# Second cross-attention of a two-layer decoder: its scores moved to the end of the odd slots, and the row minima of four heads taken together at the head of the next slot

## The chip, the cores and the metric

One core of a Trainium2 chip runs the whole program; the other cores are idle. The metric is the device time of one execution in microseconds, as a median over runs. Five engines work side by side, each through its own list of instructions in order: TensorE (PE, with its weight loads PEld), VectorE (DVE), ScalarE (ACT), GpSimd (POOL) and SyncE (SP), which issues the DMAs. They meet only at semaphores. Matmul results go to PSUM, which has eight banks; VectorE and ScalarE read them from there.

## The reference, cut to what matters

A decoder of two layers works on x of 8 batch rows x 256 positions x 512 and a context of the same shape. Each layer has a self-attention, an attention on the context and a feed-forward part, each followed by a residual addition and a layer norm. The change lies in the second layer's attention on the context, for a batch row:

```python
q = _w8a8_linear(x, wq, bq).reshape(B, N, H, D).transpose(0, 2, 1, 3)     # H = 16 heads, D = 32
k = (cond @ wk.T + bk).reshape(B, L, H, D).transpose(0, 2, 1, 3)
v = (cond @ wv.T + bv).reshape(B, L, H, D).transpose(0, 2, 1, 3)
scores = jnp.einsum('bhnd,bhld->bhnl', q, k) * inv_sqrt_d + mask[:, None]
attn = jax.nn.softmax(scores, axis=-1)
o = jnp.einsum('bhnl,bhld->bhnd', attn, v)
return _w8a8_linear(o.transpose(0, 2, 1, 3).reshape(B, N, C), wo, bo)
```

`_w8a8_linear` rounds its input by rows and its weights to whole steps of 1/127 of their largest value, multiplies, and scales back. For one batch row the scores of a head are 256 x 256.

## The kernel before, in words

The stage is `cross1`. Its work is written as a plan: a list of slots, eight for each batch row j, and in each slot a list of pieces of work. `put(slot, order, what, j, i)` places a piece; inside a slot the pieces stand by their order number. Every engine walks the same plan and, for each piece, issues its own instructions of it, or none. So one order number sets the place of a piece in all five queues. Work on row j is prepared in the slots before `base = 8 * j` (keys, rounded queries, projection, values), its attention runs in slots `base` to `base + 8`, and its output is finished up to slot `base + 17`. In a steady slot, pieces of three batch rows thus lie side by side.

The names that matter, with their lines in the profile, for row j:

- `scores` (TensorE, L2488): 24 small matmuls for four heads, into PSUM banks 0 to 3, which always hold scores. They need the exponentials of the four heads before (`s_exp`), which read the same banks. They stand in the odd slots.
- `soft`, for two heads i: VectorE adds the mask and takes the row minimum of the negated scores (L2710, four instructions and four reads of the accumulator), ScalarE takes the exponential with the minimum as bias and sums it (L2592, four). It stands in every slot.
- `flip`, for two heads: TensorE transposes the exponentials into two banks (L2501, eight), ScalarE copies them out (L2603, one instruction, 128x1024). It stands one slot behind its `soft`.
- `pv` ("attended", L2513, 16 matmuls for four heads), with ScalarE's copy (L2609); `fin` (L2523, transposes of the attended values) and `quotient` (VectorE, L2723); `round_o`, `turn_o` (L2532, copy L2615), `out` (L2542) and `out_end` (VectorE, L2742, then GpSimd).
- `key`, i = 0 to 3 (L2439, 12 matmuls), `key_high` (ScalarE, L2570), `key_low` (VectorE, L2673); `value` (L2451, 12 matmuls) and `value_out` (VectorE, L2682); `round` (VectorE, L2628 and two small ones, then GpSimd), `turn` (L2461, copy L2577), `scale` (L2424) and `scale_out` (L2662), `project` (L2472) and `project_out` (VectorE, L2696, then GpSimd).
- `n1` to `n4`: the layer norm of four tiles after every second batch row (statistics L200, normalising L232).

In the steady part the odd slot after an even one holds, besides soft, flip and scores (m is a whole number): slot 8m+1 `project_out`, `key_low`, `out`, `pv`, `key`; slot 8m+3 `project_out`, `key_low`, `fin`, `pv`, `quotient`; slot 8m+5 `value_out`, `turn_o`, `pv`, `scale`; slot 8m+7 `value_out`, `out`, `pv`, `key`. The even slots: 8m `round`, `key_low`, `key`, `project`; 8m+2 `key_low`, `key`, `project`; 8m+4 `round_o`, `value`, `turn`; 8m+6 `scale_out`, `value`.

PSUM banks other than those of the scores are handed out by `Rooms`, at build time, in the order of the plan: a piece that takes a bank waits (`left`) for the reader of the piece that had it last. Four banks serve flips and everything else, and a flip takes two. Worked out for the steady part this gives, among others: the flip of an odd slot (even i) waits for the copy of the flip one slot before; `out` in slot 8m+1 and `fin` in slot 8m+3 take the bank of the flip in their own slot and wait for its copy, and so does the `pv` of slots 8m+1 and 8m+5, and the `key` of slot 8m+7; `project` in slot 8m takes the bank of key 0 and waits for its `key_low`, which stands in the same slot; `project` in slot 8m+2 waits for the `key_low` of key 2, in that slot too; `out` in slot 8m+7 waits for `scale_out`, and the `pv` there for `value_out`.

Of the kernel before, what the change touches and what calls it, by code (L numbers as in the profile page):

```python
# [2201 lines left out]
def cross1(K):  # L2202
# [5 lines left out]
    J, U = 8, 4  # L2208
# [46 lines left out]
    def put(slot, order, what, j, i=0):  # L2255
        at.setdefault(slot, []).append((order, len(at), (what, j, i)))
# [10 lines left out]
    for j in range(J):  # L2267
        base = 8 * j
        put(base - 16 if j != 1 else -11, 6 if j != 1 else 8, "context", j)
        put(base - 16 + (j == 2), 3, "round", j)  # L2270
        first = 3 if j == 0 else -3 if j == 1 else 0
        put(base - 13 if j else 2, 6 if j else 8, "bias", j)
        put(base - 12 - first, 5, "turn", j)
        put(base - 12 - first, 9, "turned", j)
        put(base - 11 - first, 5, "scale", j)
        put(base - 10 - first, 3 if j != 1 else 1.6, "scale_out", j)
        for i in range(4):
            put(base - 9 + i - (5, 0, 0)[min(j, 2)], 5, "key", j, i)
            put(base - 8 + i - (5, 0, 0)[min(j, 2)], 1.5, "key_high", j, i)
            put(base - 8 + i - (5, 0, 0)[min(j, 2)], 4, "key_low", j, i)  # L2280
        for i in (0, 1):
            put(base - 8 + 2 * i if j else i - 10, 5, "project", j, i)
            put(base - 7 + 2 * i if j else i - 9, 2 if j == 0 else 1.7 if j == 1 else 3, "project_out", j, i)
            put(base - 6 + 2 * i if j else i - 8, 3 if j else 2.2, "project_low", j, i)
            put(base - 4 + 2 * i if j else i - 8, 5 if j else (5.5, 2)[i], "value", j, i)
            put(base - 3 + 2 * i if j else -7, 3 if j else 9, "value_out", j, i)
        put(base - 4 if j else -16, 6, "mask", j)
        for i in range(8):
            if U == 2 or i % 2 == 0:
                put(base + i - 1 if j or i else -7, 2.5, "scores", j, i // (U // 2))  # L2290
            put(base + i, 1, "soft", j, i)
            put(base + i + 1, 2, "flip", j, i)
        for g in range(4):
            put(base + 2 * g + 3, 5, "pv", j, g)
            put(base + 2 * g + 3, 9, "pv_out", j, g)
        put(base + 11, 5, "fin", j)
        put(base + 11, 9, "quotient", j)
        put(base + 12, 3, "round_o", j)
        put(base + 13, 5, "turn_o", j)
        put(base + 13, 9, "turned_o", j)  # L2300
        for i in (0, 1):
            put(base + 15 + (2 * i if j < 7 else 0), 5, "out", j, i)
            put(base + 15 + (2 * i if j < 7 else 0), 9, "out_end", j, i)
        if j % 2:
            for i, what in zip({5: (24, 24, 25, 26), 7: (16, 16, 16, 16)}.get(j, (22, 23, 26, 29)), ("n1", "n2", "n3", "n4")):
                put(base + i, 3, what, j)
# [314 lines left out]
    def vector(e):  # L2621
# [12 lines left out]
        for slot in plan:  # L2634
            for what, j, i in slot:
# [54 lines left out]
                elif what == "project_out":  # L2690
# [5 lines left out]
                        last = e.scalar_tensor_tensor(out=QF[:, m, :], in0=PS[:, b, 256 * (m % 2):256 * (m % 2) + 256],  # L2696
                                                      scalar=swI[:, m:m + 1], in1=sxB[:, :], op0=ALU.mult, op1=ALU.mult)
                    last.then_inc(p_dq.sem, 1)
                elif what == "soft":
                    n = 8 * j + i  # L2700
                    if i == 0:
                        e.wait_ge(*mk_neg.upto(j + 1))
# [182 lines left out]
    K.at_context, K.at_weights, K.at_split, K.at_exps = at_context, at_weights, at_split, at_exps  # L2885
    K.context_read, K.scores_made = x_lo.upto(J - 2), s_in.upto(16 // U * J)
    return Stage(last - first, banks, tensor, scalar, vector, gpsimd, sync)


# [344 lines left out]
def decoder(nc, d, out):  # L3234
    with ExitStack() as ctx:
# [5 lines left out]
        K.rooms, rooms = Rooms(), K.rooms  # L3241
        a1 = whole(attention1(K))
        x1 = cross1(K)
        e1 = experts1(K)
        stages = [first, a0, c0, e0, a1, x1, e1]
# [88 lines left out]
```

## Time and profile before

| | before |
|---|---|
| median of 3 runs | 2325.73 us (2324.29 to 2326.95) |
| the profiled execution's own time | 2325.44 us |
| its span | 2323.7 us |
| mean granted clock of TensorE | 0.96 |
| TensorE matmuls | 2099.0 us busy, 90% of the span |
| VectorE | 1274.0 us, 55% |
| ScalarE | 1036.9 us, 45% |
| GpSimd | 890.5 us, 38% |

The span is the time from the first to the last instruction in the profile; the execution's own time has 1.7 us more around it. The stage with the change lies at the end: its scores run from 1921.7 to 2232 us. Busy times of matmuls are modelled and overlap a little, so the time that a group of matmuls costs is best read as the distance from its start to the start of the next. A bracket behind a row of the timeline is the engine's idle time before it and the instruction whose end released it.

### The profile page before, as it was taken

The numbers are of one execution on the slowest core, as the hardware profiler recorded it, in microseconds if no ns is written. First come the engines' busy times: TensorE is split into PE (matmuls) and PEld (weight loads), VectorE is DVE, ScalarE is ACT, GpSimd is POOL, SyncE is SP. The second block draws the span as 40 slices with busy tenths as digits, with TensorE's granted clock in tenths as the row PEclk, the third lists the DMA queues.
The fourth block names the chain that finished last, engine by engine and source line by source line (L and its number), as shares of the span: only waits on it lengthen the run. The fifth ranks groups of instructions, "written<-read, shape, count | busy, mean of one in ns | idle before, by whom it ended". The sixth has DMA issues, their size and how long they took to land.

```text
span 2323.7 us, 37777 instructions
## 1 busy us (share of the span) xinstructions
PE 2099.0 (90%) x13677; PEld 1668.7 (72%) x13677; DVE 1274.0 (55%) x3279; ACT 1036.9 (45%) x2324; POOL 890.5 (38%) x944
## 2 busy tenths in 40 slices
PE   7799999899999987999999999968999877888877
PEld 6688888687777866887777788856565446667645
DVE  2554445554555455644537521146787756667767
ACT  3332333444434433444543322234666545677753
POOL 1753444334343322214433025434545335445302
PEclk9899999899999998999999999988999978999988
DMA  3302101111111111111111011103423310000001
GB/s 128 137 32 68 46 33 50 46 42 46 49 46 46 37 39 63 34 35 53 46 37 37 19 37 55 46 19 59 64 49 59 101 64 15 15 28 6 15 1 73
DMA packets 58312, 109.05 MB, mean 47 GB/s; under 512 B 7184, under 2 KB 35088, under 8 KB 54672
## 3 DMA queue, kind: packets, MB, share of 16 engines
q1 hardware_dynamic: 58128, 106.63, 15.6%
q8 instruction: 111, 1.82, 0.3%
q14 instruction: 73, 0.60, 0.1%
HBM read 86.10 MB, written 4.26 MB: 39 GB/s over the span
## 4 chain that ended last, share of the span: by engine, by line
PE 43%; DVE 10%; ACT 6%; issue 3%; POOL 2%; DMA 0%; SPq 0%; ACTq 0%; DVEq 0%; POOLq 0%
PE PS L1330 18%; ACT xP L2592 3%; PE PS L1827 3%; PE PS L1923 3%; PE PS L1346 2%; DVE aM L2063 2%; PE PS L1891 1%; DVE st L200 1%; DVE PS L2710 1%; PE PS L2451 1%; PE PS L993 1%; PE PS L2488 1%; PE PS L1911 1%; PE PS L1005 1%; PE PS L1878 1%
## 5 line engine op out<-in xcount | busy, mean ns | idle before, releaser
L1330 PE MATMUL PS<-WH,bXH 128*128 128x512 f32 x640 | 258.4, 404 | 0.0
L1330 PE MATMUL PS<-WH,bXL 128*128 128x512 f32 x640 | 250.2, 391 | 0.0
L1330 PE MATMUL PS<-WL,bXH 128*128 128x512 f32 x640 | 250.2, 391 | 0.0
L2063 DVE TENSOR_REDUCE aM<-PS 128x4 f32<-128x1024 f32 x128 | 153.8, 1221 | 55.2 <-PE PS L1891 53.9
L1627 POOL TENSOR_TENSOR mixed<-mixed,s 128x256 f32<-128x256 f32 x112 | 82.3, 739 | 234.1 <-DVE s L1528 234.0
L1632 POOL TENSOR_TENSOR WL<-sg,WH 128x512 fp32r<-128x512 f32 x80 | 101.9, 1304 | 181.7 <-ACT WH L1446 181.7
L421 PE MATMUL PS<-aXH,QKH 128*128 128x512 f32 x384 | 157.2, 409 | 14.9 <-ACT sq L634 7.9
L421 PE MATMUL PS<-aXH,QKL 128*128 128x512 f32 x384 | 153.0, 398 | 0.0
L421 PE MATMUL PS<-aXL,QKH 128*128 128x512 f32 x384 | 152.9, 398 | 0.0
L2002 ACT ACTIVATE aPT<-PS 128x1024 f32<-128x1024 f32 x128 | 128.6, 1024 | 49.4 <-PE PS L1911 48.6
L721 DVE TENSOR_TENSOR qkL<-PS,qkH 128x512 fp32r<-128x512 f32 x96 | 65.9, 690 | 142.7 <-ACT qkH L598 142.7
L1330 PEld LDWEIGHTS PS<-WH,bXH 128*128 128x128 f32 x640 | 120.5, 188 | 28.6 <-issue 2.0
L1330 PEld LDWEIGHTS PS<-WH,bXL 128*128 128x128 f32 x640 | 120.4, 188 | 26.5
L1330 PEld LDWEIGHTS PS<-WL,bXH 128*128 128x128 f32 x640 | 120.7, 189 | 22.6
L690 DVE TENSOR_TENSOR xN<-PS,xN 128x512 f32<-128x512 f32 x128 | 88.2, 691 | 78.0 <-PE PS L454 75.6
L794 POOL TENSOR_SCALAR E<-lgB,lgS 128x256 f32<-128x256 f32 x64 | 73.2, 1144 | 150.2 <-DVE aT L747 140.7
L2592 ACT ACTIVATE xP<-PS,xM 128x256 f32<-128x256 f32 x256 | 118.0, 481 | 24.6 <-DVE xM L2710 24.6
L747 DVE TENSOR_TENSOR aT<-sq,E 128x512 f32<-128x512 f32 (+1 forms) x128 | 81.6, 678 | 82.3 <-ACT sq L634 43.6
L1528 DVE SCALAR_TENSOR_TENSOR s<-s,cf,PS 128x256 f32<-128x256 f32 x112 | 53.9, 481 | 127.5 <-ACT s L1464 125.4
L598 ACT ACTIVATE qkH<-PS 128x512 fp32r<-128x512 f32 x96 | 57.1, 598 | 140.2 <-PE PS L421 140.2
L1511 DVE SCALAR_TENSOR_TENSOR s<-s,PS 128x256 f32<-128x256 f32 x80 | 33.7, 421 | 149.1 <-ACT s L1462 149.0
L804 POOL TENSOR_TENSOR E<-E,DM 128x256 f32<-128x256 f32 x64 | 45.9, 738 | 180.2 <-ACT E L609 180.2
(407 smaller groups left out, 6069.2 us busy)
## 6 DMA issues: line engine op xcount, KB each, us to landing
sg<-in_gu SPq DMA_DIRECT2D x16, 1024.0 KB, 4.8
gQK<-in_Wqk SPq DMA_DIRECT2D x16, 768.0 KB, 6.2
gC<-in_Wc SPq DMA_DIRECT2D x16, 512.0 KB, 6.4
lgB<-gate_sums SPq DMA_DIRECT2D x32, 256.0 KB, 4.6
aqs<-aQH SPq DMA_DIRECT2D x64, 128.0 KB, 4.3
xN<-in_xT SPq DMA_DIRECT2D x4, 1024.0 KB, 11.7
xN<-in_x SPq DMA_DIRECT2D x4, 1024.0 KB, 7.4
cst<-in_cT SPq DMA_DIRECT2D x8, 512.0 KB, 3.9
```

Source lines behind the costliest of these rows:

```text
L421: mm = e.matmul(PS[:, b, :], w[:, kc, 128 * m:128 * m + 128], x[:, kc, c:c + 512], start=kc == 0 and i == 0, stop=kc == KC - 1 and i == 2)
L690: e.tensor_tensor(xN[:, t, :], PS[:, b, :], xN[:, t, :], ALU.add).then_inc(o_add.sem, 1)
L747: at = e.tensor_tensor(aT[:, j, c:c + w].rearrange("p (h q) -> p h q", h=2), sq[:, c:c + w].rearrange("p (h q) -> p h q", h=2), E[:, j:j + ...
L794: e.tensor_scalar(E[:, j, 0:256], lgB[:, n % 2, 256 * j:256 * j + 256], lgS[:, c0:c0 + 1], 0.0, ALU.subtract, ALU.min)
L1330: mm = e.matmul(PS[:, b, :], x[:, kc, c:c + 128], y[:, kc, :], start=kc == 0 and n == 0, stop=kc == KC - 1 and n == 2)
L1627: e.tensor_tensor(mixed[:, i, :], mixed[:, i, :], s2[tick % 2][:, :], ALU.add).then_inc(t_add.sem, 1)
L1632: last_ = e.tensor_tensor(WL[w % 2][:, kc, :], sg[:, kc, :], WH[w % 2][:, kc, :].bitcast(F32), ALU.subtract)
L1827: mm = e.matmul(PS[:, b, 0:256], w[:, kc, 128 * m:128 * m + 128], x[:, kc, :], start=kc == 0 and k == 0, stop=kc == KC - 1 and k == 2)
L1923: mm = e.matmul(PS[32 * r:32 * r + 32, b, :], V[y][:, kt, 4 * i + r, :], PT[:, (n + 2 * (r // 2) + kt) % 8, r % 2, :], start=kt == 0, stop ...
L2002: e.activation(PT[:, n % 8, :, :], PS[:, b:b + 2, :], ACTF.Exp, scale=0.25).then_inc(t_exp.sem, 1)
L2063: e.tensor_reduce(M[j % 2][:, :, :].rearrange("x q (h c) -> x h q c", h=2)[:, :, :, i], PS[:, b:b + 2, :].rearrange("p h (q k) -> p h q k" ...
L2592: last = e.activation(P[:, i % 2, a, q, :], PS[:, r, 256 * q:256 * q + 256], ACTF.Exp, bias=M[y][:, q, h:h + 1], scale=-1.0, accum_out=den ...
```

## The change

Three order numbers in the plan and one name. `scores` gets 9.5 in place of 2.5, so that it stands last in its odd slot (the very first scores of the stage stay where they are). The minima of VectorE leave `soft` for a piece of their own, `max`, which stands for both i of an even and odd pair at 0.2 at the head of the even slot: VectorE takes the minima of four heads in one go. `key_high` of keys 0 and 2 from the third batch row on gets 0.6, ahead of the exponentials. ScalarE's part of `soft` stays.

```diff
--- before.py
+++ after.py
@@ -2276,7 +2276,7 @@
         put(base - 10 - first, 3 if j != 1 else 1.6, "scale_out", j)
         for i in range(4):
             put(base - 9 + i - (5, 0, 0)[min(j, 2)], 5, "key", j, i)
-            put(base - 8 + i - (5, 0, 0)[min(j, 2)], 1.5, "key_high", j, i)
+            put(base - 8 + i - (5, 0, 0)[min(j, 2)], 0.6 if j >= 2 and i % 2 == 0 else 1.5, "key_high", j, i)
             put(base - 8 + i - (5, 0, 0)[min(j, 2)], 4, "key_low", j, i)
         for i in (0, 1):
             put(base - 8 + 2 * i if j else i - 10, 5, "project", j, i)
@@ -2287,7 +2287,8 @@
         put(base - 4 if j else -16, 6, "mask", j)
         for i in range(8):
             if U == 2 or i % 2 == 0:
-                put(base + i - 1 if j or i else -7, 2.5, "scores", j, i // (U // 2))
+                put(base + i - 1 if j or i else -7, 9.5 if j or i else 2.5, "scores", j, i // (U // 2))
+            put(base + i - i % 2, 0.2, "max", j, i)
             put(base + i, 1, "soft", j, i)
             put(base + i + 1, 2, "flip", j, i)
         for g in range(4):
@@ -2696,7 +2697,7 @@
                         last = e.scalar_tensor_tensor(out=QF[:, m, :], in0=PS[:, b, 256 * (m % 2):256 * (m % 2) + 256],
                                                       scalar=swI[:, m:m + 1], in1=sxB[:, :], op0=ALU.mult, op1=ALU.mult)
                     last.then_inc(p_dq.sem, 1)
-                elif what == "soft":
+                elif what == "max":
                     n = 8 * j + i
                     if i == 0:
                         e.wait_ge(*mk_neg.upto(j + 1))
```

In slot 25, for instance, the order was soft, key_high, flip, scores, project_out, key_low, out, pv, key, out_end, pv_out. It becomes soft, key_high, flip, project_out, key_low, out, pv, key, out_end, pv_out, scores.

## Rows read from the trace of the kernel before

**Rows 1.** Stretch: us, busy PE, PEld, DVE, ACT, POOL, clock, DMA; slots 15 to 55.

```profile
2009.00:2202.90 193.90, 170.86 (x1732) 134.36 (x1732) 137.49 (x480) 137.84 (x419) 92.90 (x89) 1.00 0.05 17
```

**Rows 2.** Waits, 1923 to 2240 us; waited for: us, times, longest.

```profile
PE PS L2488 <- ACT xP L2592: 26.8, 26, 3.0
```

**Rows 3.** Timeline of TensorE (start, us, engine, line; wait before in brackets).

```profile
2056.55 0.39 PE L2488 MATMUL PS<-xKH,xQH 32*128 32x256 f32 x4 [0.77 <-ACT xP L2592]
...
2057.84 1.04 PE L2542 MATMUL PS<-ow,oT 128*128 128x512 bf16 x4 [0.30 <-ACT xPT L2603]
...
2059.80 0.38 PE L2439 MATMUL PS<-xXH,xWKH 128*128 128x256 f32 x1
...
2062.12 0.36 PE L2439 MATMUL PS<-xXH,xWKH 128*128 128x256 f32 x1
...
2064.52 1.04 PE L2501 MATMUL PS<-idF,xP 128*128 128x128 f32 x8
...
2066.31 0.39 PE L2488 MATMUL PS<-xKH,xQH 32*128 32x256 f32 x4 [0.75 <-ACT xP L2592]
...
2067.59 1.09 PE L2523 MATMUL PS<-idF,xnT 128*128 128x128 f32 x8 [0.30 <-ACT xPT L2603]
...
2070.59 0.48 PE L2451 MATMUL PS<-xWVH,xXH 128*128 128x512 f32 x1
...
2075.28 1.09 PE L2501 MATMUL PS<-idF,xP 128*128 128x128 f32 x8 [0.80 <-ACT qxT L2577]
...
2077.10 0.39 PE L2488 MATMUL PS<-xKH,xQH 32*128 32x256 f32 x4 [0.73 <-ACT xP L2592]
...
2086.26 0.39 PE L2488 MATMUL PS<-xKH,xQH 32*128 32x256 f32 x4 [0.99 <-ACT xP L2592]
...
2095.68 0.39 PE L2488 MATMUL PS<-xKH,xQH 32*128 32x256 f32 x4 [0.78 <-ACT xP L2592]
...
2117.00 0.39 PE L2488 MATMUL PS<-xKH,xQH 32*128 32x256 f32 x4 [0.73 <-ACT xP L2592]
...
2125.22 0.39 PE L2488 MATMUL PS<-xKH,xQH 32*128 32x256 f32 x4
```

**Rows 4.** Timeline of ScalarE.

```profile
2060.64 0.47 ACT L2592 ACTIVATE xP<-PS,xM 128x256 f32<-128x256 f32 x1 [0.25 <-DVE xM L2710]
...
2064.33 0.47 ACT L2592 ACTIVATE xP<-PS,xM 128x256 f32<-128x256 f32 x1 [0.48 <-DVE xM L2710]
...
2066.14 0.48 ACT L2570 ACTIVATE xKH<-PS,bk 128x256 fp32r<-128x256 f32 x1
...
2066.49 1.04 ACT L2603 ACTIVATE xPT<-PS 128x1024 f32<-128x1024 f32 x1
```

**Rows 5.** Timeline of VectorE.

```profile
2059.68 0.42 DVE L2710 CUSTOM_DVE_ANT_0 PS<-PS,xmk 128x256 f32<-128x256 f32 x1
...
2079.63 2.47 DVE L200 BATCH_NORM_STATS2 st<-xN 128x6 f32<-128x512 f32 x4
...
2090.51 1.22 DVE L2628 TENSOR_REDUCE sx<-xN 128x2 f32<-128x1024 f32 x1
...
2092.33 0.49 DVE L2673 SCALAR_TENSOR_TENSOR xKL<-PS,bk,xKH 128x256 fp32r<-128x256 f32 x1 [0.20 <-ACT xKH L2570]
...
2113.99 3.67 DVE L232 TENSOR_SCALAR xN<-xN,mv,ny 128x512 f32<-128x512 f32 x4
```

**Rows 6.** Timeline of TensorE behind a long wait.

```profile
1988.08 0.59 PE L2488 MATMUL PS<-xKH,xQH 32*128 32x256 f32 x4 [3.01 <-ACT xP L2592]
...
1993.20 1.09 PE L2501 MATMUL PS<-idF,xP 128*128 128x128 f32 x8
```

**Rows 7.** Timeline of TensorE, scores of slots 51, 55 and 61.

```profile
2183.92 0.39 PE L2488 MATMUL PS<-xKH,xQH 32*128 32x256 f32 x4 [0.88 <-ACT xP L2592]
...
2202.89 0.39 PE L2488 MATMUL PS<-xKH,xQH 32*128 32x256 f32 x4 [0.55 <-ACT xP L2592]
...
2231.28 0.39 PE L2488 MATMUL PS<-xKH,xQH 32*128 32x256 f32 x4 [1.85 <-ACT xP L2592]
```

## Prediction

> **What bounds the kernel now.** I read the stretches first, then the waits, then the timeline of one pass over a batch row (j), engine by engine. Between 2009 and 2203 us the second cross-attention is in its steady pattern and TensorE is busy 88% of the time at full clock [rows 1]: near its bound, with short pauses. The waits say where: its scores wait for ScalarE's exponentials, 26.8 us in 26 waits over the stage [rows 2], and the exponentials in turn wait for VectorE's minima [rows 4]. The timeline shows the loop. Starts of scores lie 9.76, 10.79, 9.16 and 9.42 us apart (slots 25, 27, 29, 31, 33); the 9.16 is 8.22 where no layer norm stands in it (2117.00 to 2125.22) [rows 3]. In one such pair of slots: scores take some 0.93 us; the output product follows, which VectorE must drain before it looks at minima; the minima begin at 2059.68, 3.1 us after the scores began; four exponentials; again minima; four exponentials to 2066.14; then the next scores at 2066.31 [rows 3 to 5].
>
> The second thing to see is the 0.30 us wait of TensorE right behind scores, at 2057.84 and 2067.59, for the PSUM copy of the flip [rows 3]. The product that stands there (out, or fin) takes the bank that the flip just before the scores has filled. ScalarE copies that bank only behind the slot's own four exponentials and a key's high part: exponentials 2064.33 to 2066.14, copy 2066.49, TensorE free at 2067.59 [rows 3, 4]. The 0.93 us of scores, plus the wait, exactly cover this copy. That cover is what the edit takes away.
>
> **The change, part by part.** No instruction is added or removed and no DMA; only orders change. (The bank plan follows flip, key, project and so on, whose order among each other stays, so every bank is the same as before.) I walk each kind of slot pair from T = 0, the end of scores, with durations of rows 3 to 5. Common head: minima begin at 0.1; exponentials of the even slot start when the first head's two minima are out, 0.96 later (2059.68 to 2060.64 [rows 4, 5]), so 1.07; four, 1.81 (2064.33 to 2066.14 [rows 4]), end at 2.88. All eight minima at 0.38 end at 3.16 instead of 1.6, which is the price of taking four heads together. The copy of the odd flip runs 2.88 to 3.93. The odd slot's exponentials no longer wait for minima: 3.93 to 5.74. A key's high part 0.36, the copy of the even flip 1.04. So TensorE may pass the bank at 7.2 with a key in the slot and at 6.84 without. Moving the high part of keys 1 and 3 of four ahead of the exponentials costs nothing: ScalarE is idle there.
>
> Slots 8m+2, 8m+3: TensorE's flip 0.8, key and project 2.4 (2062.12 to 2064.52), flip again end about 5.3 (project waits for VectorE's low part until 3.6). Then it stands until 7.2; fin and attended 2.0 (out and attended are 1.96, 2057.84 to 2059.80), scores 0.93: 10.15. Before 9.76. **+0.4**, five times, one with 0.3 more: 2.3.
>
> Slots 8m+4, 8m+5: flip 0.8, then value and turn 4.69 to the next flip with its wait (2070.59 to 2075.28, the wait for the turned copy stays as ScalarE again gets there behind the odd copy): flip ends 6.2. Copy of the even flip: exponentials 5.28 to 7.1, copy to 8.15. Attended, scale product, scores: 10.6. Before 10.79. **-0.2**, three times. Where the four normalising passes of 3.67 us [rows 5] stand ahead of the value copy, VectorE now starts them 1.5 us later against the same TensorE work: 11.9, or +1.2 once. Together 0.6.
>
> Slots 8m+6, 8m+7: copy of the even flip done at 6.79, key 1.51, scores: 9.3 against 8.2, **+1.0**, twice. With a norm's statistics (2.47 [rows 5], and I put 1.0 for its small steps and the scale's copy) VectorE, already held until 3.16 by eight minima, releases the scale at 6.7 and the value at 8.2: 11.6 against 9.16, +2.4, twice. Together 6.8. The two pairs of slots 52 to 55, 18.97 us now [rows 7], hold normalising passes and no key: 11.4 + 7.7, +0.2.
>
> Slots 8m, 8m+1: the worst. Project takes the bank of the key just before, which is freed by that key's low part, and VectorE has in front of it eight minima (to 3.16) and the rounding scale (from 2090.51, so that the low part came at 2092.33 [rows 5]; 1.6 of it is the scale), so project runs from 5.2 instead of 2.3. Then project 0.9, flip 0.8 with its 0.2 of latency, copy 7.2 to 8.25, out and attended 1.96, key 1.5, scores 0.93: 12.6 against 9.42. **+3.2**, five times: 16.0.
>
> The steady part sums to 2.3 + 0.6 + 6.8 + 0.2 + 16.0 = +25.9. In the first fifteen slots the same walk gives losses of the same kinds and gains where odd minima stood behind long VectorE work (the 3.01 us wait at 1988.08 [rows 6]); I take +1.5, bounds -5 and +8. In the tail there is little for TensorE to do and out and attended leave the loop: 28.39 us for three pairs [rows 7] become 24.5 (6.9, 8.8, 8.8). Behind the last scores both exponential groups end 5.7 later by the head above, where now two copies of the turn and one of attended stand before them; I estimate 2.7 gained. Sum at full clock: 25.9 + 1.5 - 3.9 - 2.7 = +20.8.
>
> **The clock.** Waits of up to 1 us never lowered it in the steady part [rows 1, 3]. A wait of 3.01 us at 1988.08 did: scores, fin and attended up to the flip at 1993.20 took 5.12 [rows 6] against 2.95 for the same three, so 2.2 us. The changed slots 8m, 8m+1 have one wait of 2.9 us and another of 1.3, six times with the one at slot 8. I take the fall each time: 6 x 2.1 = +12.6 (2.1 because project and flip, not all of the later work, run slow). Bounds: nothing, or every kind of pair that gets waits of 1.4 and 1.9 us as well, some 10 more at 1.5, +28 in all.
>
> The Trainium skill (TensorE: Matmul & The Clock Gate, section "A second HAM failure mode: psum-queue depth-cycling") tells of a kernel in which frequent small pauses between groups of matmuls, while banks are recycled, made the clock swing between its two levels, at a cost to throughput. The steady part here has such pauses and stays at 1.00, so as it stands the rule is not borne out; with pauses two to three times as long it speaks against the change, and is the second rival.
>
> Total +33.4 on the profiled execution's own time of 2325.44 (span 2323.7 and 1.7 around it; the median of three is 2325.73, 0.3 above): **2359 us**.
>
> **Rivals.** (1) The same walk, but the clock holds: +21, 2346. For it: the two waits of slots 8m, 8m+1 are parted by work of 1.7 us. Chance 0.2. (2) The clock swings in all pairs with pauses: 21 + 28 = +49, 2374. For it: two waits in each such pair; against it: waits of 1.4 to 1.9 us are half of the one that lowered it. 0.13. (3) Faster: TensorE's waits for exponentials go and nothing takes their place. Place: the bank that out and fin take. Price: -26.8, 2299. It decides if ScalarE gets through eight exponentials, a copy, a key and another copy (7.2 us from the scores' end) before TensorE has worked off the even slot and a flip, which needs 4.1 to 6.2 us by rows 3; so it would need ScalarE a third faster. Against it too: the present 0.30 waits. 0.06. (4) The gains of earlier odd exponentials balance the losses, because VectorE's minima overlap better than I have it: within 5 us. 0.06. My own case has 0.55.
>
> Slower by over 0.2% (4.7 us, about what a measurement of this kernel can tell from no change): 0.88; within: 0.06; faster: 0.06. Range: from the case where project is not held (pairs 8m at 11.5, no clock fall: +21 - 6.6, 2340) with something for the start of the stage, 2336, up to rival 2 with a little more, 2380.
>
> **What would show it.** In the changed trace: no wait of scores for exponentials in the steady part; instead out, fin and attended wait for the flip's copy, 1.5 to 2.5 us each in slots 8m+2, and 1.3 in 8m; project waits about 3 us for the key's low part in slots 8, 16, 24, 32, 40, 48; starts of scores 12.6 (14.7 with the clock down), 10.15, 10.6, 9.3 us apart; ScalarE's odd exponentials follow the copy without a gap; TensorE's busy share in the steady part down from 88% to about 78%; granted clock below 1.00 there. The stage's tail, from slot 55, shorter. The prediction is wrong if out and fin find their bank free, if the low part comes in time, or if the clock stays at 1.00 (then only the last term falls).

## The result and the profile after

The changed kernel takes 2369.01 us (median of 4 executions, 2366.80 to 2370.77) against 2325.01 us (4 executions, 2324.11 to 2326.95) for the kernel before. The ratio is 1.0185, 95% interval 1.017 to 1.02: slower by 44.0 us. The profiled execution has a span of 2369.0 us, against 2323.7.

In kernel.py of the changed kernel every line from the plan on stands one line further down, so its number is one higher: scores L2489, flip L2502, project L2473, out L2543, the exponentials L2593, the copy of a flip L2604, `key_low` L2674, the minima L2711. First the stretches, as in [rows 1]: slots 15 to 55.

```profile
2015.97:2249.54 233.57, 182.89 (x1707) 140.96 (x1716) 133.34 (x480) 137.68 (x417) 93.03 (x88) 0.93 0.04 13
```

The same instructions fill 233.57 us instead of 193.90. TensorE is busy 78% of it (182.89 / 233.57; 88% before), and its clock is 0.93 instead of 1.00. Its busy time itself grew by 12 us, though no matmul was added. The growth lies in the pairs of slots whose clock was below 1.00: slots 24, 25 were busy 8.63 us before and are busy 10.08 us now, at 0.88. GpSimd and ScalarE are busy for the same time as before, VectorE for 4 us less.

Second, what TensorE waited for between 1923 and 2290 us (us in total, times, longest):

```profile
PE PS L2473 <- DVE xKL L2674: 26.1, 13, 2.8
PE PS L2502 <- ACT xP L2593: 8.5, 4, 2.2
PE PS L2524 <- ACT xPT L2604: 8.0, 6, 1.5
PE PS L2543 <- ACT xPT L2604: 7.8, 6, 1.7
PE PS L2514 <- ACT xPT L2604: 7.4, 8, 1.6
```

The 26.8 us of scores behind exponentials [rows 2] are gone, to the last one. In their place project waits 26.1 us for a key's low part, and out, fin and attended wait 23.2 us for the copy of a flip.

Third, the timeline of TensorE over the pair of slots 24, 25 and the first half of the next, to be laid beside [rows 3]:

```profile
2060.68 0.39 PE L2489 MATMUL PS<-xKH,xQH 32*128 32x256 f32 x4
...
2066.93 1.89 PE L2473 MATMUL PS<-qxT,qw 128*128 128x256 bf16 x8 [2.81 <-DVE xKL L2674]
2068.61 1.59 PE L2502 MATMUL PS<-idF,xP 128*128 128x128 f32 x8
2071.61 0.81 PE L2543 MATMUL PS<-ow,oT 128*128 128x512 bf16 x3 [1.40 <-ACT xPT L2604]
...
2074.97 0.39 PE L2489 MATMUL PS<-xKH,xQH 32*128 32x256 f32 x4
...
2079.57 1.05 PE L2473 MATMUL PS<-qxT,qw 128*128 128x256 bf16 x8 [1.16 <-DVE xKL L2674]
...
2082.99 1.09 PE L2524 MATMUL PS<-idF,xnT 128*128 128x128 f32 x8 [1.50 <-ACT xPT L2604]
```

Project and the flip behind it in slot 24 of the kernel before, which [rows 3] don't have:

```profile
2053.86 1.05 PE L2472 MATMUL PS<-qxT,qw 128*128 128x256 bf16 x8
2054.74 1.04 PE L2501 MATMUL PS<-idF,xP 128*128 128x128 f32 x8
```

The changed kernel's stretch on VectorE and on ScalarE:

```profile
2061.85 0.43 DVE L2711 CUSTOM_DVE_ANT_0 PS<-PS,xmk 128x256 f32<-128x256 f32 x1 [2.84 <-PE PS L2489]
...
2064.88 1.21 DVE L2629 TENSOR_REDUCE sx<-xN 128x2 f32<-128x1024 f32 x1
...
2066.41 0.47 DVE L2674 SCALAR_TENSOR_TENSOR xKL<-PS,bk,xKH 128x256 fp32r<-128x256 f32 x1
```

```profile
2060.85 0.47 ACT L2571 ACTIVATE xKH<-PS,bk 128x256 fp32r<-128x256 f32 x1 [1.21 <-PE PS L2440]
2062.84 0.48 ACT L2593 ACTIVATE xP<-PS,xM 128x256 f32<-128x256 f32 x1 [1.52 <-DVE xM L2711]
...
2064.66 1.03 ACT L2604 ACTIVATE xPT<-PS 128x1024 f32<-128x1024 f32 x1
2065.56 0.49 ACT L2593 ACTIVATE xP<-PS,xM 128x256 f32<-128x256 f32 x1
...
2070.30 1.02 ACT L2604 ACTIVATE xPT<-PS 128x1024 f32<-128x1024 f32 x1 [2.42 <-PE PS L2502]
```

Read them from the end of scores, at 2061.60. VectorE works through eight minima to 2064.88, then through the rounding scale, and gets to the low part of the key at 2066.41. Project takes the bank that this instruction frees and stands still for 2.81 us. ScalarE's exponentials of the odd slot follow its copy without a gap (2065.56), and it is done with them at 2067.4 and with a key's high part at 2067.9. Then it waits 2.42 us for the flip, which is late because project was. So the two waits of TensorE are in series, and the rows of project and flip (1.89 and 1.59 in place of 1.05 and 1.04) show the clock at the lower of its levels between them.

The starts of scores lie 14.29 (slots 24, 25), 10.04, 10.82, 12.84, 16.75 and 12.54 us apart, against 9.40, 9.76, 10.79, 9.16, 9.42 and 10.54 before.

### The profile page after: what moved, and what is told of

Its sections match the earlier page's. It is cut to its first block, busy times and chain, and to the rows that moved or that the text cites. A ratio compares the mean times of both kernels' runs of the same rounds, so it can differ in the third digit from the quotient of the medians.

```text
span 2369.0 us, 37756 instructions
## 1 busy us (share of the span) xinstructions
PE 2112.5 (89%) x13663; PEld 1676.6 (71%) x13677; DVE 1267.2 (53%) x3279; ACT 1038.7 (44%) x2324; POOL 893.2 (38%) x944
## 4 chain that ended last, share of the span: by engine, by line
PE 43%; DVE 10%; ACT 5%; issue 4%; POOL 2%; SPq 1%; DMA 1%; ACTq 0%; DVEq 0%; POOLq 0%
PE PS L1330 17%; PE PS L1923 3%; PE PS L1827 3%; PE PS L1346 2%; DVE st L200 2%; DVE aM L2063 1%; ACT xP L2593 1%; DVE PS L2711 1%; PE PS L1891 1%; PE PS L2502 1%; PE PS L2514 1%; PE PS L2440 1%; ACT xPT L2604 1%; PE PS L2489 1%; PE PS L993 1%
## 5 line engine op out<-in xcount | busy, mean ns | idle before, releaser
L421 PE MATMUL PS<-aXH,QKH 128*128 128x512 f32 x384 | 157.1, 409 | 15.4 <-ACT sq L634 7.9
L2711 DVE CUSTOM_DVE_ANT_0 PS<-PS,xmk 128x256 f32<-128x256 f32 x256 | 99.4, 460 | 96.8 <-PE PS L2489 96.8
L2593 ACT ACTIVATE xP<-PS,xM 128x256 f32<-128x256 f32 x256 | 118.5, 488 | 50.5 <-PE PS L2502 32.9
```

The lines of the kernel that those rows point to most:

```text
L421: mm = e.matmul(PS[:, b, :], w[:, kc, 128 * m:128 * m + 128], x[:, kc, c:c + 512], start=kc == 0 and i == 0, stop=kc == KC - 1 and i == 2)
L2593: last = e.activation(P[:, i % 2, a, q, :], PS[:, r, 256 * q:256 * q + 256], ACTF.Exp, bias=M[y][:, q, h:h + 1], scale=-1.0, accum_out=den ...
L2711: last = e.tensor_tensor_reduce(out=s, in0=s, in1=mk[y][:, q, :], scale=1.0, scalar=3.0e38, op0=ALU.add, op1=ALU.min, accum_out=M[y][:, q, ...
```

## The experiments

Each change below is against the changed kernel or the kernel before, as said; diffs show the plan's lines. Ratios are to the kernel before, measured on the same chip.

### 1. low_first: `key_low` ahead of the minima

Added to the changed kernel.

```diff
-put(base - 8 + i - (5, 0, 0)[min(j, 2)], 4, "key_low", j, i)
+put(base - 8 + i - (5, 0, 0)[min(j, 2)], 0.1 if j >= 2 and i % 2 == 0 else 4, "key_low", j, i)
```

> The changed kernel with one order number more: key_low of keys 0 and 2 (from the third batch row on) at 0.1, ahead of the four heads' minima on VectorE. If the project of slots 8m is held by VectorE's queue, as the walk has it, these pairs (14.3 to 14.5 us in the changed kernel, one 16.75) become 11.6, slot 35 falls from 12.5 to about 10.9, slots 8m+2 stay at 10.0, and the whole is some 20 us shorter than the changed kernel: 2349. If only the PSUM copies hold TensorE, the wait moves behind the flip and the time stays at 2369; if the clock falls as before in spite of the shorter wait (2.4 in place of 2.8 us), about 2358.

Measured: 2362.56 us, ratio 1.0158 (1.0143 to 1.0173). Project's wait is gone from slots 24, 25, but those slots still take 13.34 us. The timeline of TensorE there, scores' end at 2056.71:

```profile
2059.07 1.05 PE L2473 MATMUL PS<-qxT,qw 128*128 128x256 bf16 x8
2060.86 1.09 PE L2502 MATMUL PS<-idF,xP 128*128 128x128 f32 x8 [0.73 <-ACT xPT L2604]
2063.96 1.69 PE L2543 MATMUL PS<-ow,oT 128*128 128x512 bf16 x4 [2.01 <-ACT xPT L2604]
2065.58 1.94 PE L2514 MATMUL PS<-xPT,xV 128*32 128x256 f32 x16
```

The stretch from scores to scores, with its clock:

```profile
2055.80:2069.14 13.34, 10.59 (x93) 7.20 (x92) 7.08 (x24) 6.82 (x21) 7.28 (x8) 0.87 0.01 2
```

What follows: out stands until 7.25 us behind the scores' end, where ScalarE's four exponentials, copy, four exponentials, high part and copy end (7.2 in the prediction). ScalarE's row of work is a second limit right behind VectorE's, and removing the first alone saves about 1 us a pair, where 2.7 to 2.9 were expected. Behind the 2.01 us wait the clock was down too: out and attended took 1.69 and 1.94. In slots 8, 9 of the same execution, where it stayed at 1.00, the pair took 11.33 us, near the 11.6 of the walk.

### 2. fill_wait: work put where project waits

Added to the changed kernel: key 1 of a row (from the third row on) multiplies its 12 products three times over into its bank, so 24 matmuls more in slots 8m, with the same result. They lie in the stretch where project would wait.

```diff
-for kc in range(KC):
+for _ in range(3 if j >= 2 and i == 1 else 1):
+    for kc in range(KC):
```

> The changed kernel, but TensorE does the 12 matmuls of key 1 in slots 8m three times into the same bank (the same result), which fills 2.8 us of the 2.8 us wait for the key's low part; nothing else is moved. If the fall of the clock behind this wait is a cost of its own, the pairs of slots 8m go from 14.3 to 12.6 us (the one of 16.75 too), and the kernel is some 10 to 13 us faster than the changed one in spite of 2.8 us more matmul work in each: 2357. If the clock has no part in it: 2369 or a little more.

Measured: 2361.94 us, ratio 1.0151 (1.0136 to 1.0166): with 24 matmuls more in each of six batch rows it is some 7 us faster than the changed kernel, where 10 to 13 were expected. Slots 24, 25:

```profile
2056.29:2069.23 12.94, 11.77 (x117) 9.81 (x117) 6.97 (x24) 6.92 (x21) 6.88 (x7) 1.00 0.01 2
```

The clock is at 1.00 and the pair takes 12.94 instead of 14.29, near the 12.6 of the walk. In none of the six filled pairs did it fall. So without the wait there was no fall, and one fall costs about 1.4 us a pair. Part of the gain was lost again in slots 46 to 51 (13.35, 12.85 and 13.04 against 11.80, 11.77 and 10.89): the clock was at 0.87 in the first and at 0.77 in the last of them, and in slot 48 the changed kernel's project waits only 1.29 us, so the added matmuls found no wait long enough there.

### 3. scores_early: the changed kernel with scores back at 2.5

```diff
-put(base + i - 1 if j or i else -7, 9.5 if j or i else 2.5, "scores", j, i // (U // 2))
+put(base + i - 1 if j or i else -7, 2.5, "scores", j, i // (U // 2))
```

> The changed kernel with the scores back at 2.5 in their odd slot; the minima of four heads together and the early key_high stay. If scores last is what loses the cover of the flip's copy, the waits of out and fin go back to 0.3 us or less, slots 8m+2 take about 9.1 us (9.76 in the kernel before, because the odd exponentials no longer wait for minima), slots 8m about 10.0 (9.42 before, the key's low part is late), the others as before, and the time is 2325 within 5. If the minima together are the cause of the loss: 2350 or more.

Measured: 2321.25 us, ratio 0.9981 (0.9972 to 0.9991). The whole loss is gone. The waits of out and fin are back at 0.3 us. Pairs take 9.77, 10.08 (9.1 expected), 10.78 and 8.23 us; the clock is at 1.00. The gain over before is small, and ScalarE shows why:

```profile
2054.79 0.47 ACT L2571 ACTIVATE xKH<-PS,bk 128x256 fp32r<-128x256 f32 x1 [1.16 <-PE PS L2440]
2055.17 0.47 ACT L2593 ACTIVATE xP<-PS,xM 128x256 f32<-128x256 f32 x1
```

With scores in their old place the key of the odd slot is multiplied behind them. Its high part, now ahead of the exponentials in the queue, waits 1.16 us for it, and the exponentials stand behind.

### 4. minima_apart: the changed kernel with minima in every slot again

```diff
-put(base + i - i % 2, 0.2, "max", j, i)
+put(base + i, 0.2, "max", j, i)
```

> The changed kernel with the minima again in two parts, each at the head of its own slot; scores last and the early key_high stay. By the walk slots 8m+2 stay at 10.0 us, slots 8m fall from 14.3 to 12.2 and those with a norm's statistics to about 11.4, the clock holds more often, and the time is 2353. If scores last alone makes the whole loss: 2369. If the minima together make it: near 2325.

Measured: 2374.80 us, ratio 1.0212 (1.0195 to 1.0229). Splitting the minima doesn't mend the loss; the median is higher still (the interval just overlaps that of the changed kernel, 1.017 to 1.02). The expected 2353 was a miss. Project's wait in slots 24, 25 did shrink, from 2.81 to 1.28 us, but out then waited 2.16 us for the copy of the flip instead of 1.40, the clock was at 0.88 as before, and the pair took 13.92 us where 12.2 had been expected. So taking four heads together isn't what made it slow.

### 5. early_plain: the kernel before with the minima of four heads together, nothing else

> The kernel before with one edit of the three: the minima of four heads together at the head of the even slot (scores stay early in the odd slot, key_high behind the exponentials). The two exponential groups then stand apart only by the copy and, in slots 8m and 8m+2, the key's high part of 0.36 us. If the gain of scores_early (2321.3, 3.8 under the kernel before) comes from the minima together, this one keeps all but the 0.36 us in two pairs of each batch row: 2324. If it comes from the early key_high, this one is at 2325 to 2330, since VectorE frees the projection's bank later.

Measured: 2313.55 us, ratio 0.9945 (0.9932 to 0.9957): faster than both kernels, and below both cases of the expectation. In slots 15 to 55 the wait of scores for exponentials falls from 14.3 to 4.9 us, but project's wait for the low part grows from 0.7 to 6.2 us, in six waits of up to 1.8. So that stretch gains only 3.4 us (190.5 against 193.9). Most of the gain, 8.9 us, stands in the slots before: slots 2, 3 take 8.47 us (10.90 before), slots 4, 5 take 9.85 (12.82, at a clock of 0.75, now 1.00), slots 10, 11 take 10.42 (13.54).

### 6. high_only: the kernel before with the early high part alone

> The kernel before with only key_high of keys 0 and 2 ahead of the exponentials. VectorE then does not wait for the high part between the two groups of minima (1.66 us at 2062.97 in the kernel before), the odd minima and with them the odd exponentials and the scores come up to 0.9 us earlier in slots 8m+2 and 0.4 in slots 8m: 2319. If the scores are held by ScalarE's own work and not by this wait: 2325.

Measured: 2327.89 us, ratio 1.0007 (0.9998 to 1.0016). No gain, for the reason seen in 3: the high part waits 1.21 us for the key's product, ahead of the exponentials. The expected 2319 was a miss: I had looked at ScalarE's free time and not at when the key's product is done.

### 7. early_low: scores_early with `key_low` first as well

> scores_early with key_low of keys 0 and 2 at 0.1, ahead of the four heads' minima. If the late low part holds the project of slots 8m when the minima are together, those pairs go from 9.77 to about 8.9 us and slots 8m+2 from 10.08 to about 9.1, and the whole to 2312 to 2315, faster than both kernels. If TensorE is held there by the exponentials only: 2321, as scores_early.

Measured: 2345.07 us, ratio 1.0082 (1.0068 to 1.0095), where a gain had been expected. VectorE:

```profile
2057.46 0.49 DVE L2674 SCALAR_TENSOR_TENSOR xKL<-PS,bk,xKH 128x256 fp32r<-128x256 f32 x1 [2.34 <-ACT xKH L2571]
2057.86 0.42 DVE L2711 CUSTOM_DVE_ANT_0 PS<-PS,xmk 128x256 f32<-128x256 f32 x1
```

The minima are now queued behind a low part that waits 2.34 us for the high part, which waits for the key's product. Slots 24 to 29 take 11.3, 11.6 and 11.7 us a pair, the last at a clock of 0.87. The same step that takes project's wait away where scores stand last costs 24 us where they don't.

### 8. low_copy: low_first, and ScalarE copies the even flip ahead of the odd exponentials

ScalarE's part of an even slot's flip gets a piece of its own, `copy`, at 0.9 in the odd slot; TensorE's part of the flip stays.

```diff
+            if i % 2 == 0:
+                put(base + i + 1, 0.9, "copy", j, i)
...
-                elif what == "flip":
+                elif what == "copy" or what == "flip" and i % 2:
```

> low_first (2362.6), with one piece more: ScalarE copies the flip of the even slot at 0.9 in the odd slot, ahead of the odd slot's exponentials and not behind them. If the PSUM bank of that flip is what out, fin and attended wait for (2.0 us in low_first), they may pass 1.1 us earlier, the pauses get shorter and the clock falls less: slots 8m 10.7 us (13.3 in low_first), 8m+2 9.1 (10.5 to 11.1), 8m+4 10.3, 8m+6 9.4, in all about 2336. If the wait is one for ScalarE's exponentials as such, the time stays at 2362.

Measured: 2355.22 us, ratio 1.0127 (1.0111 to 1.0142). Pairs 8m and 8m+2 take 10.92 and 9.20 us, near what was expected, out waits 1.2 instead of 2.0, and in slots 16, 24, 32 and 48 the clock stays at 1.00. In slots 40, 41 it fell all the same, to 0.86, behind the same two short waits, and the pair took 12.49 us:

```profile
2150.91 1.09 PE L2504 MATMUL PS<-idF,xP 128*128 128x128 f32 x8 [0.74 <-ACT xPT L2606]
2153.17 1.51 PE L2545 MATMUL PS<-ow,oT 128*128 128x512 bf16 x4 [1.18 <-ACT xPT L2606]
2154.61 1.94 PE L2516 MATMUL PS<-xPT,xV 128*32 128x256 f32 x16
```

But pair 8m+4 takes 11.90 (10.3 expected), because the flip there now waits for VectorE's quotient:

```profile
2081.75 1.07 PE L2504 MATMUL PS<-idF,xP 128*128 128x128 f32 x8 [1.33 <-DVE xoN L2726]
```

A partial miss: both limits of pair 8m are shown, but a third turns up in the next pair but one. With scores last, mending each queue in turn leaves 29 us of the 44.

### 9. last_plain: the changed kernel without the early high part

> The changed kernel with key_high of keys 0 and 2 back behind the exponentials: scores last and minima together. ScalarE then does the high part of 0.36 us between the even exponentials and the copy that the next flip waits for, so slots 8m and 8m+2 get 0.3 to 0.4 us longer each: 2373. If the early key_high costs in this order too, as it does with the scores early (2321.3 against 2313.6 without it, because ScalarE's exponentials stand behind a product that TensorE has not done yet): below 2365.

Measured: 2364.33 us, ratio 1.0168 (1.0154 to 1.0182), overlapping the changed kernel's. The expected 2373 was a miss: the early high part gives nothing here. Its profile was of more use than its time. Three pairs 8m with the same work (slots 16, 24, 32):

```profile
2014.17:2028.48 14.31, 10.32 (x93) 7.94 (x93) 6.98 (x24) 6.81 (x21) 8.24 (x8) 0.88 0.00 0
2059.14:2072.09 12.95, 8.96 (x94) 6.93 (x94) 6.98 (x24) 6.81 (x21) 6.88 (x7) 1.00 0.01 2
2105.11:2120.69 15.58, 11.59 (x93) 8.08 (x92) 6.97 (x24) 6.81 (x21) 9.43 (x9) 0.78 0.00 1
```

In the first two project waited the same 2.82 us. In one the clock fell, in the other not:

```profile
2020.42 1.89 PE L2473 MATMUL PS<-qxT,qw 128*128 128x256 bf16 x8 [2.82 <-DVE xKL L2674]
...
2065.39 1.05 PE L2473 MATMUL PS<-qxT,qw 128*128 128x256 bf16 x8 [2.82 <-DVE xKL L2674]
```

That gives the pair at full clock, 12.95 us, and one fall, 14.31 - 12.95 = 1.36 us.

### 10. last_only: the kernel before with scores last, nothing else

> The kernel before with one edit of the three: scores last in the odd slots. Minima stay in two parts (each at the head of its slot), key_high behind the exponentials. If scores last is the whole loss and the minima together soften it (they gain 12.5 us where the scores are early), this is the slowest of all: 2375 to 2385. If the loss needs the minima together, because only then project is held: 2340 or less.

Measured: 2375.52 us, ratio 1.0227 (1.0211 to 1.0242), as expected. The move of scores alone makes the loss, 50 us of it. Out and fin wait 2.2 us each for the copy of the flip, project 15.4 us in ten waits.

### 11. early_round: early_plain, with the rounding scale and layer norm behind the low part

```diff
-put(base - 16 + (j == 2), 3, "round", j)
+put(base - 16 + (j == 2), 4.5 if j >= 3 else 3, "round", j)
```

`n3` of the rows j < 5 goes from 3 to 4.5 in the same way.

> early_plain (2313.6: minima together alone) with the rounding scale of slots 8m and the norm's third step at 4.5, behind key_low on VectorE. In early_plain TensorE waits 0.94 us for that low part in slots 8m, which take 9.68 us against 9.14 in slots 8m+2. If VectorE's order is what holds project there, slots 8m go to 9.14 and slots 35 from 10.86 to 9.2: 2308, the fastest. If the rounding on GpSimd comes too late for the turned queries in its place, or nothing waits: 2313 or more.

Measured: 2311.05 us, ratio 0.9939 (0.9927 to 0.9952), the lowest median of all, 14.8 us below the kernel before. Pair 8m takes 8.83 us in place of 9.68 in early_plain, and slots 34, 35 take 9.17 in place of 10.86. Whether it is faster than early_plain can't be told: the intervals of their ratios overlap.

### The parts laid out

| medians, us | high part in its place | high part early |
|---|---|---|
| scores at 2.5, minima apart | 2325 to 2326 | 2327.9 |
| scores at 2.5, minima together | 2313.6 | 2321.3 |
| scores last, minima apart | 2375.5 | 2374.8 |
| scores last, minima together | 2364.3 | 2369.0 |

Scores last costs 47 to 51 us in every column. Minima together gains 11 to 13 us with the high part in its place (ratios 0.9945 against 1, and 1.0168 against 1.0227, with intervals apart). The early high part costs some 8 us beside minima together and early scores (0.9981 against 0.9945, intervals apart) and can't be told from nothing in the other rows.

## Why the prediction was right, and its terms one by one

The forecast was 2359, +33.4 on the profiled execution; the span grew by 45.3, the medians by 44.0. Sign and mechanism were right; the size was 12 us short. Both waits that the walk named are there, in the places named; experiment 1 took the first away and experiment 8 shortened the second. The sum against the profile follows. The clock's part is taken out by setting each pair beside one of the same kind that ran at 1.00, in last_plain or in the changed kernel itself (last_plain has the high part in its old place, so the split is good to some tenths). What is set at full clock is the changed kernel only: the kernel before had falls of its own, in slots 4, 5 (0.75), 12, 13 (0.81) and 58 to 61 (0.83), and its times hold them.

| term | forecast | measured |
|---|---|---|
| 8m, 8m+1, at full clock | +16.0 | +16.5 |
| 8m+2, 8m+3 | +2.3 | +1.9 |
| 8m+4, 8m+5 | +0.6 | +1.4 |
| 8m+6, 8m+7 | +6.8 | +7.7 |
| slots 52 to 55, at full clock | +0.2 | +0.4 |
| first fifteen slots, at full clock | +1.5 | +5.6 |
| tail, at full clock | -3.9 | -3.8 |
| behind the last scores | -2.7 | -0.7 |
| clock | +12.6 | +16.3 |
| sum | +33.4 | +45.3 |

**The steady walk** came out at 27.9 against 25.9. Four pairs 8m are set at 12.95 at full clock against a forecast 12.6 (3.5 each over the old time), the fifth at 11.77, where project waits only 1.29 us because no rounding scale stands ahead of the low part: in slot 48 the forecast had put the same queue as in the others. The norm pairs take 11.80 at full clock (11.6 forecast), the pair of slots 36, 37 takes 12.07 (11.9).

**The first slots** were mis-sized most. Of the +7.0 measured up to slot 15, 1.7 arose before the stage's first scores, ahead of anything that the change touches (other kernels here began them between 1919.5 and 1924.7 us). The pair of slots 8, 9 cost 5.5, as the walk gives with its clock (3.2 + 2.1). I had set gains of nearly the same size against it for odd minima that no longer stand behind long VectorE work; slots 2 to 5 and 10, 11 gave back 5.4 and slots 0, 1, 6, 7, 14 and 15 took it again. This term was an estimate from one row [rows 6], not a walk. The gains it hoped for belong to the minima together and are there (8.9 us where scores stay early, experiment 5); scores last outweighs them.

**The tail.** In last_plain its three pairs take 7.10, 8.64 and 8.84 us, 24.6 together, where the walk said 6.9, 8.8 and 8.8. In the changed kernel they take 8.72, 8.64 and 10.34, because the clock fell twice behind waits of the even flip for the exponentials. The clock was low in slots 54, 55 too, behind a wait for VectorE's value copy (8.85 us against 7.79 in last_plain). What was mis-sized is the clock's term: I charged the clock to the pairs 8m alone. TensorE in slots 52 to 61:

```profile
2238.99 0.66 PE L2533 MATMUL PS<-idF,qtmp 128*128 128x128 f32 x4 [2.39 <-DVE xV L2683]
...
2242.27 1.83 PE L2502 MATMUL PS<-idF,xP 128*128 128x128 f32 x8
...
2253.78 1.70 PE L2502 MATMUL PS<-idF,xP 128*128 128x128 f32 x8 [2.23 <-ACT xP L2593]
2255.70 1.49 PE L2543 MATMUL PS<-ow,oT 128*128 128x512 bf16 x3 [0.22 <-issue]
...
2262.34 1.06 PE L2502 MATMUL PS<-idF,xP 128*128 128x128 f32 x8 [2.07 <-ACT xP L2593]
...
2270.98 1.82 PE L2502 MATMUL PS<-idF,xP 128*128 128x128 f32 x8 [2.07 <-ACT xP L2593]
```

**Behind the last scores** 0.7 us was gained, not 2.7. The clock hardly differs (0.89 before, 0.87 after, 0.88 in last_plain, which has 92.0 us there against 91.8 after and 92.4 before). What takes the place of the earlier exponentials wasn't traced and stays open.

**The clock.** Forecast: six falls of 2.1. Measured: one fall costs some 1.4, but there were more and one long one. (The 2.1 was somewhat too large already by the rows that it came from: the same three groups take 3.16 us at full clock without their wait, from 2066.31 to the flip at 2069.77 less 0.30, and not 2.95.) By pair: 1.5, 1.3 and 1.4 (slots 16, 24, 40), 3.8 (slots 32, 33, where it stayed down from project at 2114.92 to the key at 2123.96), 1.0 (30, 31), 1.6 (34, 35), 1.1 (54, 55), 3.1 in the tail, and some 1.4 for slots 8, 9 by the clock of 0.88 there; in slots 48, 49 none. The three long steps in a row, slots 30 to 35:

```profile
2103.72 1.33 PE L2543 MATMUL PS<-ow,oT 128*128 128x512 bf16 x3 [1.89 <-DVE sxB L2663]
...
2114.92 1.89 PE L2473 MATMUL PS<-qxT,qw 128*128 128x256 bf16 x8 [2.81 <-DVE xKL L2674]
2116.59 1.92 PE L2502 MATMUL PS<-idF,xP 128*128 128x128 f32 x8
2120.09 1.49 PE L2543 MATMUL PS<-ow,oT 128*128 128x512 bf16 x3 [1.58 <-ACT xPT L2604]
...
2131.20 1.89 PE L2473 MATMUL PS<-qxT,qw 128*128 128x256 bf16 x8 [2.35 <-DVE xKL L2674]
```

The trace before had also more to say on the clock than the one wait of 3.01 us. In its tail the clock fell behind pairs of waits of 1.8 and 1.6 us, rows that the prediction didn't look at when it called waits of 1.4 to 1.9 us half of what had lowered it:

```profile
2218.64 1.06 PE L2501 MATMUL PS<-idF,xP 128*128 128x128 f32 x8 [1.81 <-ACT xP L2592]
...
2221.28 0.39 PE L2488 MATMUL PS<-xKH,xQH 32*128 32x256 f32 x4 [1.58 <-ACT xP L2592]
...
2222.64 1.97 PE L2523 MATMUL PS<-idF,xnT 128*128 128x128 f32 x8
```

**The early high part** "costs nothing: ScalarE is idle there" is right for the changed kernel (2060.85 above, with 1.52 us idle behind it). It hangs on scores being last: with scores in their old place the same edit puts a wait of 1.16 us ahead of the exponentials (3).

**The rivals.** (1), the clock holds, is excluded by the rows and by experiment 2. (2), the clock swings in all pairs with pauses, holds in part: it fell outside 8m as well, but pairs 8m+2 with waits of 1.16 and 1.50 us stayed at 1.00. (3), faster, fell with its condition: ScalarE needs 7.25 us from the end of scores (1). (4), balance: the gains of earlier exponentials exist and belong to the minima together, but they are 11 to 13 us, with scores early (5) or last (9 against 10), and scores last costs four times that.

The Trainium skill (TensorE: Matmul & The Clock Gate, section "A second HAM failure mode: psum-queue depth-cycling") says that small frequent pauses while banks are recycled can make the clock swing. The trace after agrees: 0.93 over slots 15 to 55 with pauses up to 2.8 us, where the trace before, with pauses up to 1 us, had 1.00. So in the steady stretches of these two traces the swing came with the longer pauses; low_copy's slots 40, 41, where the clock fell behind 0.74 and 1.18 us, show that short pauses can be enough (8).

## What to carry to other kernels

What stands between a producer and its consumer on a full engine is often the cover for something else: here out, attended and key behind scores gave TensorE work while minima and exponentials ran, and scores put last took this cover away, for 47 to 51 us. Before an instruction is moved in an in-order queue, ask of each bank when its reader comes up in the reader's own queue, and of each instruction moved ahead when its input will be ready; an engine that is idle at that place is no answer (3, 6, 7). When an edit has parts, run them apart: this one held a gain of 11 to 13 us inside a loss of 44.

## What the runs showed of the hardware

- Waits of one length don't always do the same to TensorE's clock. Behind 2.82 us it fell once and held once in one execution (9); behind 2.07 us it held at 2262.34 and fell at 2270.98; behind 1.89 us it fell at 2103.72 and held in slot 47 (11.80 us at 1.00). Short waits aren't safe either: behind 0.74 and 1.18 us it held in four pairs 8m of low_copy and fell in the fifth (8). What the engine did before each wait differs, and what of that decides was not tested.
- One fall costs little by itself, 1.36 us for a pair of 13, as most of the work at the low clock is project and flip (1.05 to 1.89, 1.04 to 1.59). In slots 32, 33 the next wait (1.58 us) came before the clock was back, and it stayed down: 3.8 us for that pair.
- More work can be faster: 24 matmuls more in each of six batch rows, put into a wait, took the kernel from 2369.0 to 2361.9 us (2).
